# Layer norm of the LSTM's rows written by ScalarE instead of VectorE, with a new order of the engines' queues

## What is computed

```python
h = relu(einsum('ts,bsh->bth', adj, x @ Wg0 + bg0))
h = relu(einsum('ts,bsh->bth', adj, h @ Wg1 + bg1))
for p in range(1, 5):                     # windows of p nodes
    wins = h[:, :nw * p, :].reshape(Bv * nw, p, Hd)
    last = _lstm_last(Wih[p-1], Whh[p-1], bih[p-1], bhh[p-1], wins)
    h = h.at[:, arange(nw) * p + (p - 1), :].set(last)
x = layernorm(x + h)                      # (x - mean) / sqrt(var + 1e-5), per row
...
agg = einsum('nm,bmd->bnd', A_hat, x)
h = relu(batchnorm(agg @ W1.T + b1))
out = batchnorm(h @ W2.T + b2)
x = layernorm(x + out)
```

## Time and profile before

| | us |
|---|---|
| median of 3 runs | 840.4 (840.08 to 840.74) |
| the profiled execution | 839.27 |
| its span, first to last instruction | 837.5 |
| TensorE busy | 805.8 |
| VectorE busy | 704.6 |
| ScalarE busy | 593.3 |
| GpSimd busy | 68.9 |

### The profile page before, as it was taken

How to read it: one execution, slowest core, us unless ns; L and a number is a source line. 1 busy time by engine, 2 the same in 40 slices (tenths; PEclk the granted TensorE clock), 3 DMA queues, 4 the chain that set the end, 5 groups by cost and what they waited for, 6 DMA issues and landing times.

```text
span 837.5 us, 15410 instructions
## 1 busy us (share of the span) xinstructions
PE 805.8 (96%) x4872; PEld 517.8 (62%) x4872; DVE 704.6 (84%) x1795; ACT 593.3 (71%) x1186; POOL 68.9 (8%) x58
## 2 busy tenths in 40 slices
PE   8999999999999999999999999999999977999984
PEld 7667677567757765776567657765675653333542
DVE  5678989888988898898889888998989986677995
ACT  4777777767776677767776777677776762990498
POOL 0000000000000000000000000000000001000674
PEclk9999999999999999999999999999999999999998
DMA  6000010201120012001100110011010110344244
GB/s 214 29 26 2 1 55 22 76 1 36 43 77 0 25 50 75 0 25 50 63 12 25 50 45 31 26 51 51 1 51 2 51 41 36 100 142 133 77 163 188
DMA packets 17691, 44.94 MB, mean 54 GB/s; under 512 B 2032, under 2 KB 3184, under 8 KB 17520
## 3 DMA queue, kind: packets, MB, share of 16 engines
q1 hardware_dynamic: 17648, 44.39, 14.9%
HBM read 27.61 MB, written 16.78 MB: 53 GB/s over the span
## 4 chain that ended last, share of the span: by engine, by line
PE 77%; issue 9%; DVE 9%; ACT 3%; SPq 1%; POOL 0%; DMA 0%; ACTq 0%; DVEq 0%; POOLq 0%
PE gate_bank L812 15%; PE gate_bank L813 15%; PE gate_bank L797 9%; PE gate_bank L828 6%; PE gate_bank L838 6%; PE back_bank L770 3%; PE front_bank L735 3%; PE front_bank L741 3%; PE front_bank L729 3%; PE front_bank L724 3%; DVE bn L1022 3%; PE gate_bank L821 3%; ACT z L940 2%; PE back_bank L778 1%; PE back_bank L780 1%
## 5 line engine op out<-in xcount | busy, mean ns | idle before, releaser
L812 PE MATMUL gate_bank<-h_hi,w_hi 128*128 128x256 f16 (+2 forms) x528 | 165.2, 313 | 5.1 <-DVE h_lo L1115 4.8
L813 PE MATMUL gate_bank<-h_hi,w_lo 128*128 128x256 f16 (+2 forms) x528 | 164.6, 312 | 0.0
L890 ACT ACTIVATE gate_i<-gate_bank,lstm_bias 128x256 f32<-128x256 f32 (+2 forms) x176 | 99.9, 572 | 71.1 <-PE gate_bank L838 58.7
L890 ACT ACTIVATE gate_o<-gate_bank,lstm_bias 128x512 f32<-128x512 f32 (+2 forms) x176 | 99.7, 571 | 35.5 <-PE gate_bank L838 21.1
L828 PE MATMUL gate_bank<-h_lo,w_hi 128*128 128x256 f16 (+2 forms) x384 | 117.7, 306 | 0.0
L1099 DVE SCALAR_TENSOR_TENSOR gate_f<-gate_o,gate_f 128x512 f32<-128x512 f32 (+2 forms) x176 | 95.1, 540 | 23.7 <-ACT gate_f L896 22.9
L812 PE MATMUL gate_bank<-s_hi,w_hi 128*128 128x256 f16 (+2 forms) x384 | 112.5, 301 | 0.5 <-DVE s_hi L1112 0.5
L813 PE MATMUL gate_bank<-s_hi,w_lo 128*128 128x256 f16 (+2 forms) x384 | 112.4, 301 | 0.0
L890 ACT ACTIVATE gate_g<-gate_bank,lstm_bias 128x256 f32<-128x256 f32 (+2 forms) x176 | 100.2, 569 | 6.3 <-PE gate_bank L838 3.3
L838 PE MATMUL gate_bank<-s_lo,w_hi 128*128 128x256 f16 (+2 forms) x384 | 102.4, 302 | 0.0
L896 ACT ACTIVATE gate_f<-cell 128x512 f32<-128x512 f32 (+2 forms) x176 | 88.8, 510 | 16.2 <-DVE cell L1090 9.8
(11 more groups left out here) (162 smaller groups left out, 1573.3 us busy)
## 6 DMA issues: line engine op xcount, KB each, us to landing
x_front<-in_x SPq DMA_DIRECT2D x16, 512.0 KB, 4.4
rows_sb<-in_x SPq DMA_DIRECT2D x16, 512.0 KB, 3.3
x_kept<-normed_sb SPq DMA_DIRECT2D x16, 512.0 KB, 2.7
z<-x_kept SPq DMA_DIRECT2D x16, 512.0 KB, 3.6
out<-z SPq DMA_DIRECT2D x15, 512.0 KB, 3.1
z<-in_wr SPq DMA_DIRECT2D x1, 1536.0 KB, 6.5
out<-z SPq DMA_DIRECT2D x2, 256.0 KB, 2.2
wih_sb<-in_wih SPq DMA_DIRECT2D x1, 192.0 KB, 2.4
```

The source lines that it names most:

```text
L812: mm(dst, w[0], v[0], start=start, stop=False)
L813: mm(dst, w[1], v[0], start=False, stop=False)
L890: ins = activation(acts[gate][h][:, 0:n], gate_bank[h][bank_of(job, gate)][:, 0:n], ACT.Tanh if gate == "g" else ACT.Sigmoid, bias=lstm_bi ...
```

## The change

Layer norm of a half: VectorE keeps one small step, `shift`, which computes -mean*rstd for the 8 graphs once `rstd` is there. Then ScalarE writes the normalized rows, with rstd as scale and the shift as bias, eight instructions in two blocks of four. The waits for the write-back move from VectorE to ScalarE with it. TensorE's `mix` and SyncE's write wait for `normed` as before; its semaphore is now raised by ScalarE. The planner gets the new operations with costs, and the dependency of the second job's gate o that the kernel has already. The table `AHEAD_OP` is replaced as a whole: 74 entries before, 114 after, so that the order of nearly all queues differs.

```diff
@@ lstm_stage @@
         for gate in gates:
-            ops.append(("ACT", (job, "act", gate), scalar_us(n, 1), [(job, "gate", gate)]))
+            after = [(LSTM_JOBS[0], "hidden")] if gate == "o" and job == LSTM_JOBS[1] else []
+            ops.append(("ACT", (job, "act", gate), scalar_us(n, 1), [(job, "gate", gate)] + after))
@@ back_stage @@
     ops.append(("POOL", ("back", "rstd"), 1.62, [("back", "moments", 2)]))
+    ops.append(("DVE", ("back", "shift", 0), 0.08, [("back", "rstd")]))
     for n in range(2):
-        ops.append(("DVE", ("back", "normed", n), 1.02, [("back", "rstd")]))
+        ops.append(("ACT", ("back", "normed", n), 4 * scalar_us(P, 2), [("back", "shift", 0)]))
@@ AHEAD_OP @@
-    ('PE', 'front', ('lin1', 'product', 0, 2)): -0.15,
...
-    ('DVE', 'back', ('back', 'z_stats', 3)): 0.15,
+    ('PE', 'front', ('mix0', 'product', 0, 0)): -0.6,
+    ('ACT', 'front', ('mix0', 'out', 0)): -1.3,
...
+    ('DVE', 'back', ('back', 'shift', 0)): 0.15,
+    ('ACT', 'back', ('back', 'normed', 0)): -0.8,
+    ('ACT', 'back', ('back', 'normed', 1)): -1.2,
...
+    ('ACT', 'back', ('back', 'z_stored', 3)): -0.75,
@@ block.scalar, emit @@
+                    if what == "normed":
+                        if n == 0:
+                            wait(act, ("back", "shift", 0), g, h)
+                            if not isinstance(g, int):
+                                act.wait_ge(sem_kept, loads(g, h, -16))
+                            elif 2 * g + h > 0:
+                                act.wait_ge(sem_kept, 16 * (2 * g + h))
+                        for b in range(4 * n, 4 * n + 4):
+                            at = slice((b % 4) * P, (b % 4 + 1) * P)
+                            ins = activation(normed[:, n, at], rows[:, n, at], ACT.Identity,
+                                             bias=mean_rstd[0][:, b:b + 1], scale=rstd[0][:, b:b + 1])
@@ block.vector @@
-            def normalize(src, dst, comb_t, rstd_t, n):
-                for b in range(4 * n, 4 * n + 4):
-                    at = slice(b * P, (b + 1) * P)
-                    last = ve.tensor_scalar(flat(dst[:])[:, at], flat(src[:])[:, at], comb_t[:, 2, b:b + 1],
-                                            rstd_t[:, b:b + 1], ALU.subtract, ALU.mult)
-                return last
...
-                elif what == "normed":
-                    if n == 0:
-                        wait(dve, ("back", "rstd"), g, h)
...
-                    ins = normalize(rows, normed, comb[0], rstd[0], n)
+                elif what == "shift":
+                    wait(dve, ("back", "rstd"), g, h)
+                    ins = ve.scalar_tensor_tensor(out=mean_rstd[0][:], in0=comb[0][:, 2, :], scalar=-1.0,
+                                                  in1=rstd[0][:], op0=ALU.mult, op1=ALU.mult)
```

More of the change, by code:

```diff
@@ new lines @@
+    ('PE', 'front', ('mix1', 'product', 1, 0)): -0.95,
+    ('PE', 'even', (('lstm', 1, 0), 'gate', 'i')): -0.9,
+    ('ACT', 'even', (('lstm', 1, 0), 'act', 'o')): -1.4,
+    ('DVE', 'even', (('lstm', 1, 0), 'hidden')): -0.8,
+    ('DVE', 'even', (('lstm', 1, 0), 'high')): -0.65,
+    ('DVE', 'even', (('lstm', 1, 0), 'low')): -0.9,
+    ('PE', 'even', (('lstm', 1, 1), 'gate', 'i')): -0.3,
+    ('PE', 'even', (('lstm', 1, 1), 'gate', 'o')): -0.6,
+    ('ACT', 'even', (('lstm', 1, 1), 'tanh')): -0.55,
@@ new lines @@
+    ('ACT', 'even', (('lstm', 3, 0), 'act', 'i')): -0.65,
+    ('ACT', 'even', (('lstm', 3, 0), 'act', 'o')): -1.0,
+    ('PE', 'even', (('lstm', 3, 1), 'input', 'i')): -0.05,
+    ('PE', 'even', (('lstm', 3, 1), 'high', 'i')): -0.75,
+    ('PE', 'even', (('lstm', 3, 1), 'high', 'g')): -1.1,
+    ('PE', 'even', (('lstm', 3, 1), 'input', 'o')): -0.6,
+    ('DVE', 'even', (('lstm', 3, 1), 'hidden')): -0.6,
+    ('ACT', 'even', (('lstm', 3, 2), 'act', 'i')): -0.4,
+    ('ACT', 'even', (('lstm', 3, 2), 'tanh')): -1.65,
@@ new lines @@
+    ('DVE', 'even', (('lstm', 3, 2), 'high')): -0.9,
+    ('PE', 'even', (('lstm', 4, 0), 'gate', 'i')): -1.0,
+    ('DVE', 'even', (('lstm', 4, 0), 'new')): -0.8,
+    ('ACT', 'even', (('lstm', 4, 0), 'tanh')): -1.3,
+    ('PE', 'even', (('lstm', 4, 1), 'input', 'i')): -0.55,
+    ('PE', 'even', (('lstm', 4, 1), 'input', 'g')): -0.55,
+    ('PE', 'even', (('lstm', 4, 1), 'gate', 'o')): -0.4,
+    ('ACT', 'even', (('lstm', 4, 1), 'act', 'i')): -1.55,
+    ('PE', 'even', (('lstm', 4, 2), 'input', 'i')): -0.75,
@@ new lines @@
+    ('ACT', 'odd', (('lstm', 1, 1), 'act', 'o')): -0.75,
+    ('ACT', 'odd', (('lstm', 1, 1), 'tanh')): -1.05,
+    ('DVE', 'odd', (('lstm', 1, 1), 'low')): -0.25,
+    ('ACT', 'odd', (('lstm', 2, 0), 'act', 'g')): -1.35,
+    ('DVE', 'odd', (('lstm', 2, 0), 'hidden')): -0.6,
+    ('PE', 'odd', (('lstm', 2, 1), 'high', 'i')): -0.7,
+    ('PE', 'odd', (('lstm', 2, 1), 'gate', 'o')): -0.7,
+    ('ACT', 'odd', (('lstm', 2, 1), 'act', 'i')): -1.8,
+    ('DVE', 'odd', (('lstm', 2, 1), 'new')): -0.7,
@@ new lines @@
+    ('ACT', 'odd', (('lstm', 2, 1), 'tanh')): 1.0,
+    ('DVE', 'odd', (('lstm', 2, 1), 'hidden')): -0.85,
+    ('PE', 'odd', (('lstm', 3, 0), 'gate', 'i')): -1.05,
+    ('ACT', 'odd', (('lstm', 3, 0), 'act', 'i')): -0.8,
+    ('PE', 'odd', (('lstm', 3, 1), 'input', 'f')): -0.6,
+    ('PE', 'odd', (('lstm', 3, 1), 'input', 'o')): -1.25,
+    ('ACT', 'odd', (('lstm', 3, 1), 'act', 'i')): -0.65,
+    ('DVE', 'odd', (('lstm', 3, 1), 'cell')): -0.55,
+    ('ACT', 'odd', (('lstm', 3, 1), 'act', 'o')): -1.1,
@@ new lines @@
+    ('DVE', 'odd', (('lstm', 4, 2), 'new')): -1.25,
+    ('DVE', 'odd', (('lstm', 4, 2), 'hidden')): -0.75,
+    ('PE', 'odd', (('lstm', 4, 3), 'input', 'i')): -0.65,
+    ('ACT', 'odd', (('lstm', 4, 3), 'act', 'i')): -1.0,
+    ('ACT', 'odd', (('lstm', 4, 3), 'act', 'o')): -0.45,
+    ('PE', 'back', ('back', 'tokens', 0, 0)): -0.1,
+    ('DVE', 'back', ('back', 'stats', 0)): -0.7,
+    ('DVE', 'back', ('back', 'stats', 1)): -0.5,
+    ('DVE', 'back', ('back', 'moments', 0)): -0.55,
+    ('DVE', 'back', ('back', 'moments', 2)): -0.35,
@@ new lines @@
+    ('DVE', 'back', ('back', 'shift', 0)): 0.15,
+    ('ACT', 'back', ('back', 'normed', 0)): -0.8,
+    ('ACT', 'back', ('back', 'normed', 1)): -1.2,
+    ('PE', 'back', ('back', 'mix', 0, 0)): -0.55,
+    ('PE', 'back', ('back', 'mix', 1, 2)): -0.35,
+    ('ACT', 'back', ('back', 'mixed', 1)): -0.75,
+    ('PE', 'back', ('back', 'z', 0)): -0.5,
+    ('ACT', 'back', ('back', 'z_stored', 0)): -1.2,
+    ('DVE', 'back', ('back', 'z_stats', 0)): -0.4,
+    ('PE', 'back', ('back', 'z', 1)): -0.5,
```

117 lines of the change are left out of this document (39 added, 78 removed).

## The result

The changed kernel takes 852.9 us (median of 4 runs, 851.87 to 853.66) against 840.6 us before (840.08 to 841.2): a measured ratio of 1.0151, 95% interval 1.0137 to 1.0165 (the plain quotient of the two medians is 1.0147). It is slower by 12.3 us, where 838.2 was forecast in a range of 834.0 to 843.2. The changed table of start shifts has 106 entries, not the 114 that are stated above.

The account below looks back on a forecast made before the run. TensorE was taken to bound the loop, with VectorE's time reaching the end only between 629 and 692 us. Loop 0, tail -3.3, last half +1.1, order table 0 sum to -2.2: 840.4 to 838.2 us, range 834.0 to 843.2.

Parts of the forecast that it names:

- The loop costs nothing: Loop passes: TensorE's 84.6 us cover ScalarE's added 5.6 us and VectorE's relief, so the change is worth 0.
- the failing of the cover: Loop: if TensorE's cover fails, a 1.4 us block stands before a gate or tanh in ScalarE's queue; costed at nothing.
- The allowance of 1.2 us for hidden stalls: Loop: one stall of up to 0.17 us a pass may hide in TensorE's modelled busy time, 1.2 us in all.
- wrong if the pass gets longer: Loop: passes stay at 84.6 us; a longer pass would mean ScalarE's blocks reach TensorE and refute the prediction.
- The tail gives 3.3: Tail, about 629 to 692 us: of 5.9 us net relief of VectorE, 3.3 us reach the end.
- a little over half: Tail: the share of VectorE's 5.9 us net relief taken to reach the end, 3.3 us.
- The last half +1.1: Exposed back stage of the last half: shift, crossing and ScalarE's slower blocks delay the mix and statistics by 1.1 us.
- The order table 0, plus or minus 4: Queues of TensorE, ScalarE and VectorE: the replaced order table taken as zero, with 4 us kept each way.
- ScalarE's queue gets in the way: Rival, after 629 us: 1.4 us blocks stand ahead of the last stream's gate or tanh; +3.2, 843.6 us; chance 0.24.
- The relief doesn't arrive: Rival, tail: only 0.7 us of visible delays comes back and the last half pays 1.1; about 840.8 us; chance 0.24.
- The new order fills the tail: Rival, tail: half of TensorE's 7.4 us of holes is recovered on top of the sum; 834.5 us; chance 0.14.
- The signs: Expected to show it: passes 84.6 us, VectorE about 70, ScalarE about 68, last `low` to last `z_stats` 15.6 us.

Follow-up runs that it names:

- the padded kernel: The changed kernel with 24 one-column clearing instructions more on VectorE ahead of its loop: 849.8 us, ratio 1.0128.
- the move alone: The kernel before with its queue orders kept and only the normalizing work moved to ScalarE, VectorE keeping the shift: 875.1 us, ratio 1.0421.

## Why the prediction was wrong

**The loss, by the runs.** It is 12.3 us against the kernel before of the same measurement (840.6) and 13.2 against that of the experiments (839.7). In the third column each figure is the difference of two medians, the edits standing on one another; the last column is what the profiles show of the same thing:

| edit | what it takes away | medians, us | profiles, us |
|---|---|---|---|
| 24 instructions ahead of VectorE's loop | late return to the loop's head | 3.1 | 3.4 (three returns) |
| 16 more idle products | fall of the clock in the last half | 1.5 | 1.5 |
| table of before for the start | hole at 22 us | 2.7 | 1.9 (first `rstd`) |
| last residual from `x_front` | wait for the rows' load | 2.7 | 1.3 |
| left over | | 3.3 | 5.1 (13.2 less the four above) |

The difference between the columns goes with TensorE's clock: whether it falls in a stretch changes between executions of one kernel, and the executions of the last version have it up more often (0.994 to 0.997) than most of the kernel before (0.989 to 0.994). So each row is good to about 1 us, and 3.3 is too low for what is left: up to the power of the batch norm the last version is 6.0 us later than the kernel before (714.47 against 708.49), and only its closing phase, 127.0 us against 129.0, takes 2 us of that back.

The left-over part has no run of its own. By the table of standstills it lies in the loop, 4.4 against 1.6 us, in the tail, 13.0 against 12.2, and in the last half, 13.54 against 12.31 us.

**What ScalarE's work costs in it.** The run with three quarters of ScalarE's blocks left out cuts across these rows: it takes away 5.9 of the 10.2 us by which the padded kernel is slower than the kernel before. By the profiles 3.3 us of it lie in the last half (1.5 of them the fall of the clock), 1.2 in the tail and 0.15 us in each pass. So the work itself is over half of what remains once the return is repaired, and most of that is in the last half, where the prediction had 1.1 us for it. A pass of the padded kernel is 85.10 us against 84.65, with ten standstills of 0.06 to 0.10 us where the kernel before has three of 0.06. Two of them are at the mix behind ScalarE's block and are gone with three quarters of its work left out (84.95 us); so 0.15 of the 0.45 us is ScalarE's, and what the rest waits for stays open.

**"The loop costs nothing": wrong, the largest miss.** The step argued that TensorE's 84.6 us cover ScalarE's new 5.6 us, from busy shares. Two things got through the cover. One was not in the sum at all: taking instructions away from VectorE's program moved its loop to a place where the return takes 2.8 us. That is shown in both directions, and 16 instruction packets in the loop where the kernel before has none go with it. The other was named by the prediction as the failing of the cover (a block in front of a gate) and then priced at nothing: under the old orders it is five stalls of 0.5 to 0.7 us a pass, 2.9 us. The new table pays for most of it and not all (85.10 us without the late return). The allowance of 1.2 us for hidden stalls looked the wrong way: it asked what could be won, not what a longer block could lose. The sign that the prediction itself gave ("wrong if the pass gets longer") was the right one.

**"The tail gives 3.3": wrong in size, and not all of it was tail.** With three quarters of VectorE's block gone and nothing put on ScalarE the tail gives 0.9 us under the old orders; scaled to the whole, as an estimate, it is 1.2. The visible delays in the earlier trace rows gave 0.7 us, and that reading was nearly right; "a little over half" of VectorE's freed time was a choice with no row behind it. In the changed kernel the stretch from the loop's end to the last `rstd` is 179.2 us against 172.5, but some of this is order: its `rstd` stands at another point of a pass, so only the waits inside can be compared. The standstills can: 13.1 us against 12.2, no gain at all. One that the kernel before doesn't have is a mix of an earlier half, behind ScalarE's `normed` and `mixed` (with three quarters of ScalarE's blocks left out this wait is 0.40 us instead of 1.41):

```profile
621.64 1.13 PE L804 MATMUL back_bank<-ahatT,normed_sb 128*128 128x128 f32 x8 [1.41 <-DVE rows_sb L1107]
```

**"The last half +1.1": mechanism right, size off.** Measured +2.15. The shift took 0.17 us, as taken, and the crossing to ScalarE 0.03 instead of 0.1. The ACTIVATEs start 0.385 us apart (3.18 us less one duration of 0.49, by seven), not 0.35: +0.25. This is where the estimate from the Trainium skill (ScalarE: Activation LUTs, section What ACT_TABLE_LOAD costs) said 0.39 and the prediction went with the PSUM rows; the SBUF form agrees with the page. Most of the rest is TensorE's clock after the longer idle time, 3.81 us instead of 1.88: the second mix 2.08 us instead of 1.16. With the clock held up the stretch is 13.55, +1.24 against +1.1 predicted. The wait for the rows' load stands ahead of this stretch. It wasn't in the sum either. The load is issued when the half before has had its last z products from the same buffer, at 688.92 us before and at 701.77 in the changed kernel (SyncE's timeline). Before, that was 3.5 us ahead of the residual and hidden by it; here it comes as late as the bank, for which the last half's token products now wait too. The earlier trace rows has them wait for `h_lo`, the LSTM; here it is the statistics of the half before:

```profile
703.35 0.22 PE L792 MATMUL back_bank<-ident,h_hi 128*128 128x128 f16 x1 [1.60 <-DVE z_moments L1111]
```

So what is late at the end of the tail is no longer the last LSTM stream but the back stage of half 14. ScalarE's blocks stand in that stage, but with three quarters of their work left out the same wait is again 1.60 us, and with the old orders and less norm on VectorE it is `h_lo` with 2.18 us as before; with the new orders and the old work on VectorE it is `z_moments` with 1.60 us again. The runs put this one down to the new order.

**"The order table 0, plus or minus 4": right to keep apart, wrong in what it bounds.** New orders with the old work cost 17.7 us, the new work with old orders 35.3 (28.4 when padded). Neither is the 4 us that was allowed each way. The term with its 4 us had no row behind it, as the prediction says. A table fitted to one set of durations can't be read as a term beside the change; it belongs to it. Its own defect, a start in which ScalarE waits for work that the planner doesn't model, is 1.9 to 2.7 us.

**The rivals.** "ScalarE's queue gets in the way" had the right sign with 843.6 us, and what it named, a block ahead of a gate or mix in the tail, is there. It is a good part of the loss and not all of it: 5.9 us by the run above, but more in the last half (3.3) than in the tail (1.2), where this rival had its 2.8 us; the late return and the start come beside it. That the measured time lies beyond this rival's 843.6 is due to these. "The relief doesn't arrive" was right about the relief (839.2 with less norm). "The new order fills the tail" did not come about: last `rstd` at 700.9 us in the best of the changed versions, 696.2 before. None of the versions beat the kernel before.

**The signs.** ScalarE's busy time in a pass rose to 68.05 us (68 expected); VectorE's fell to 71.7 (70 expected), by 2.6 instead of 4.3 us. They say nothing of the time. From the last `low` to the last `z_stats` there are 20.4 us (700.69 to 721.13) where 15.6 were expected and 14.5 stood before, since the last half's tokens wait for half 14's statistics. ScalarE waited for `mean_rstd` twice, 0.48 us in the tail and 8.36 us in the last half, and never inside the loop: the blocks reached TensorE by their length and place in the queue, not by that wait.

## What to carry to other kernels

When an edit changes how many instructions an engine issues ahead of a loop, look at that engine's first instruction after the branch (seen here on VectorE alone): idle time put down to "issue" there, with more packets on the instruction queue, is a cost of the loop's place, and some idle instructions ahead of the loop (24 here) move it away. Where TensorE is the bound and its queue follows a fixed order, work moved to an engine with idle time is still not free if one block takes longer there: compare the block's duration (1.63 against 1.11 us) with the time at which the waiting product stands in the queue, not the busy shares. And take relief of an engine beside the bound at the delays that the timeline shows, not at a share of the time freed.

## What was not expected of the hardware

- VectorE's return to a loop's head takes 0.3 or about 2.8 us, by the place of the loop: 2.8 with the head at record 300 or 303, 0.3 at 315 to 331, with loops of 303 to 324 records. With the long return q14 carries 14 to 16 more packets (35 or 34 against 19 to 21), of 8 KB each: 16 of them lie between 250 and 525 us in the changed kernel, and none in the kernel before or the padded one. The Trainium skill (Runtime: NRT & Kernel Launch, section Instruction fetch mechanics) says that a taken branch with its target outside the two pages that the engine holds forces a fetch before execution goes on; the traces agree with that, but no run here shows where the pages' borders lie.
- The cost of that return isn't its own length. In the changed kernel work already in VectorE's queue covered 1.6 of the 2.8 us, and the pass lost 1.1 us; with the move alone it lost 2.0.
- TensorE's granted clock went from 2.4 to 1.2 GHz three times in the changed kernel before its last products, each time after it had stood: at the start (0.57 on average from 24 to 28 us, after 1.93 us), in the last half (0.69 from 712.3 to 716.2, after 3.81 us) and in the closing phase (0.80 from 725 to 729). Idle products in one place moved the fall elsewhere (12 in the tail of the kernel before) or removed it (16 more ahead of the last mix, in that stretch). Whether it falls isn't settled by the kernel alone: the padded kernel and the one with 16 more idle products are the same up to the last mix, both stand 1.61 us for `s_hi` in the tail, and the clock is 0.50 behind it in the second (689 to 692 us) and 1.00 in the first (687 to 691). Two executions of one kernel can differ by 3.5 us with it (843.7 at 0.996, 847.2 at 0.991).
